# Routing logits without transposes: a fused attention and mixture-of-experts layer on one core

## Chip, core and metric

One core of a Trainium2 chip runs the whole program. The time is device microseconds (us) of that core, as the median of several executions. The kernel keeps five engines busy by hand: TensorE (PE), VectorE (DVE), ScalarE (ACT), GpSimd (POOL), and SyncE (SP), which issues nearly all transfers. They meet only at semaphores.

## Reference

The input is `x` of 4 x 2048 tokens and 256 numbers a token. Everything below starts from the normalised rows.

```python
xn = layernorm(x)
attn = attention over the 16 heads of one token, with biases            # A: per token
h  = rmsnorm(xn, g1);  y = xn + softmax(q k^T) v @ Wo                   # B: causal, 16 heads
t  = rmsnorm(y, g2) = y * r * g2,   r = 1 / sqrt(mean(y*y) + 1e-6)      # C: routing
logits = t @ gate_w;  top_v, top_i = top_k(logits, 2);  gates = softmax(top_v)
moe = sum over the two chosen experts of gate * (silu(t @ w1[e]) @ w2[e])
out = x + attn + y + moe
```

## The kernel before, in words

The program has four stages, one after the other.

- **Projections** (`phase1_project`): 16 chunks of 512 tokens. A chunk is normalised, transposed through PE and projected; one of the products is `heads_ps` (query, key and value columns of part A, 3 x 256 of them, in `head_rows`), which `take_heads` on DVE scales, biases and moves to `heads`. DVE, POOL and ACT make the low parts and statistics beside it.
- **Causal attention** (`phase2_attend`): 16 units of four heads. It leaves the output `o` in memory. The last unit's division by the row sums is left over for the next stage.
- **Routing** (`route`): again 16 chunks, n = 0 to 15, on four token tiles of 128 rows each. For a chunk, PE multiplies `oT` by `wo` (`project`, into `mla_ps`), DVE adds `xn` and has `x2` (the y above), ACT squares it (`squares`), POOL makes `rrms` (the r above, `inverse_rms`), DVE scales to `th` (the t above, `scale_rms`), and ACT copies it (`copy_th`), since each row goes to two experts. Before the change PE also transposes `th` (`transpose_th`), ACT copies the transposed rows (`copy_tT`), and PE multiplies them by `gate_w` (`logits_of`). DVE then picks the two largest logits, PE counts ranks within the experts with triangular and all-ones matrices (`ranks`), DVE turns them to row positions `pos`, and POOL sends the rows to `sorted_rows` with eight indirect transfers a chunk.
- **Experts** (`experts`): 71 tiles of 256 sorted rows, each through two products, added to the output by indirect transfers.

Within routing each engine runs its own list, with work for later chunks placed in it: while chunk n is being ranked, the inputs of chunk n + 2 are made. The lists before are a loop over the first three batches (4 chunks an iteration) and a written-out last batch. The order within a list is that of the code, so a wait holds everything behind it on the same engine. SP's list holds, between the loads and the stores, the last unit's quotients (`scatter_inverse`, `load_raw`, `store_quotient`, with a multiplication of `raw` by `spread` on POOL between them) and the zero rows behind the experts' rows (`blank`).

POOL's part before the loop and in it:

```python
            inverse_rms(0)
            inverse_rms(1)
            wait_apart(pool, last_quotient, RAW_LANDED, apart)
            nc.gpsimd.tensor_tensor(raw[:, :], raw[:, :], spread[:, :], ALU.mult).then_inc(last_quotient, 1)

            def body(b, c, n, ahead):
                if ahead >= 2:
                    inverse_rms(n + 2)
                wait_apart(pool, th_copied, n + 1, apart)
                wait_apart(pool, pos_done, n + 1, apart)
```

## Time and profile before

| | us |
|---|---|
| median of 3 runs | 2802.31 (2799.14 to 2805.09) |
| profiled execution | 2787.22 |
| its span, first to last instruction | 2785.5 |
| PE busy | 2507.4 (90%) |
| DVE busy | 2173.4 (78%) |
| POOL busy | 2140.7 (77%) |
| ACT busy | 1588.1 (57%) |

Stages are read from where their instructions start. Projections run to about 411 and attention from 423.8 to 1963; routing's PE work starts at 1965.7, and the experts' first load is issued at 2217.8. Every share above is a mean over stages with different limits, so the table says nothing on what one stage is worth. That is read from the stage's own rows. In rows, p_ stands in front of tile names, p_small_ps holds the ranks, p_x is x2 in routing, p_g is g2 there, and rows_by_expert is sorted_rows.

### The profile page before, as it was taken

How to read it: one execution, taken by the hardware profiler on the slowest of the kernel's cores; microseconds unless marked ns; L12 is line 12 of the kernel's file. 1: busy time of each engine (PE TensorE's matmuls, PEld its weight loads, DVE VectorE, ACT ScalarE, POOL GpSimd, SP SyncE). 2: the span in 40 equal slices, each digit the busy share in tenths (PEclk: the TensorE clock that was granted, in tenths of full speed). 3: DMA queues.
4: the chain of work that ended last, by engine and by line, in shares of the span. 5: the costliest groups of instructions: out<-in, count | busy, mean ns of one | idle time of the engine just before them, and what ended most of it. 6: DMA issues, size and time to landing. Idle time of an engine off the chain costs nothing. (4 is left out here: it accounts for less than half of the span.)

```text
span 2785.5 us, 57388 instructions
## 1 busy us (share of the span) xinstructions
PE 2507.4 (90%) x21356; PEld 1283.6 (46%) x21356; DVE 2173.4 (78%) x3704; ACT 1588.1 (57%) x2397; POOL 2140.7 (77%) x1245
## 2 busy tenths in 40 slices
PE   7998988999999999999999999999677399999995
PEld 3554443333333333333333333322466288888884
DVE  4557868999899899989999998980266379999980
ACT  2322215677777777777777777778444245555551
POOL 5543338999999999999999999994267556676664
PEclk9999999999999999999999999999777599999997
DMA  5786553223233223322333332211586556565554
GB/s 163 243 252 202 174 174 91 59 73 91 70 86 97 63 81 88 90 73 75 95 69 88 82 91 68 69 38 36 157 280 204 166 118 132 129 133 127 132 118 83
DMA packets 235167, 324.48 MB, mean 116 GB/s; under 512 B 31544, under 2 KB 174744, under 8 KB 234392
## 3 DMA queue, kind: packets, MB, share of 16 engines
q1 hardware_dynamic: 207544, 283.08, 35.6%
q0 software_dynamic: 27360, 37.91, 7.3%
q8 instruction: 163, 2.67, 0.4%
q14 instruction: 100, 0.82, 0.1%
HBM read 238.57 MB, written 145.39 MB: 138 GB/s over the span
## 5 line engine op out<-in xcount | busy, mean ns | idle before, releaser
L1055 DVE TENSOR_REDUCE p_piece_max<-p_ring 128x1 f32<-128x512 f32 (+3 forms) x2160 | 1291.5, 653 | 135.9 <-PE p_ring L164 62.9
L1118 ACT ACTIVATE p_probs<-p_st 128x1024 f32<-128x1024 f32 (+3 forms) x1280 | 1080.7, 897 | 410.7 <-PE p_st L1181 213.9
L1181 PE MATMUL p_st<-unit_q,unit_k 64*128 64x512 bf16 (+3 forms) x3520 | 432.3, 347 | 32.7 <-ACT p_probs L1118 16.8
L1199 PE MATMUL p_pv<-p_probs,unit_vg 128*32 128x512 f32 (+3 forms) x3520 | 410.0, 540 | 0.0
L1869 POOL DMA_INDIRECT out<-p_y,p_rows x142 | 223.0, 1571 | 165.3 <-ACT p_y L1988 100.5
L985 POOL TENSOR_TENSOR p_terms<-p_head_in 128x4096 f32<-128x4096 f32 x38 | 336.1, 8845 | 4.9 <-DMA p_head_in<-head_qkv 4.8
L1012 POOL TENSOR_TENSOR p_terms<-p_head_p,p_head_in 128x4096 f32<-128x4096 f32 x38 | 335.9, 8840 | 0.0
L989 POOL TENSOR_TENSOR p_terms<-p_terms 128x2048 f32<-128x2048 f32 (+2 forms) x114 | 299.6, 2628 | 8.9
L1016 POOL TENSOR_TENSOR p_terms<-p_terms 128x2048 f32<-128x2048 f32 (+2 forms) x114 | 299.5, 2627 | 8.9
L177 PE MATMUL p_ring<-unit_k,unit_q 64*128 64x512 bf16 (+3 forms) x1600 | 271.2, 352 | 32.8 <-DVE p_piece_max L1055 30.3
L2013 PE MATMUL p_hid_ps<-p_rT,p_w 128*128 128x256 f32 x1136 | 259.9, 382 | 3.8 <-DMA p_w<-ffn_w 3.8
L2025 PE MATMUL p_y_ps<-p_w,p_hid 128*128 128x256 f32 x1136 | 257.0, 379 | 0.7 <-ACT p_hid L1976 0.7
L177 PEld LDWEIGHTS p_ring<-unit_k,unit_q 64*128 64x128 bf16 x1600 | 71.3, 93 | 368.4 <-DVE p_piece_max L1055 356.0
L2013 PEld LDWEIGHTS p_hid_ps<-p_rT,p_w 128*128 128x128 f32 x1136 | 217.9, 192 | 34.4 <-issue 4.2
L1181 PEld LDWEIGHTS p_st<-unit_q,unit_k 64*128 64x128 bf16 x3520 | 136.1, 94 | 207.9 <-ACT p_probs L1118 121.2
L2025 PEld LDWEIGHTS p_y_ps<-p_w,p_hid 128*128 128x128 f32 x1136 | 210.4, 190 | 26.6 <-issue 0.9
L1181 PE MATMUL p_st<-p_q,p_k 34*128 34x512 bf16 (+7 forms) x1600 | 194.2, 346 | 8.2 <-ACT p_probs L1118 7.1
L1199 PE MATMUL p_pv<-p_probs,p_vg 128*32 128x512 f32 (+3 forms) x1600 | 186.3, 540 | 0.0
L1856 POOL TENSOR_TENSOR p_pv<-p_pr,p_qkv 128x1024 f32<-128x1024 f32 (+2 forms) x64 | 147.7, 2308 | 30.5 <-ACT p_q_ps L1968 30.5
L1468 POOL DMA_INDIRECT rows_by_expert<-p_th,p_pos x128 | 127.5, 996 | 37.6 <-issue 37.2
L1976 ACT ACTIVATE p_hid<-p_hid_ps 128x512 f32<-128x512 f32 x142 | 84.7, 597 | 114.6 <-PE p_hid_ps L2013 114.3
L177 PE MATMUL p_ring<-p_k,p_q 64*128 64x512 bf16 (+3 forms) x800 | 135.2, 351 | 13.1 <-DVE p_piece_max L1055 11.7
(192 smaller groups left out, 3377.8 us busy)
## 6 DMA issues: line engine op xcount, KB each, us to landing
p_w<-ffn_w SPq DMA_DIRECT2D x142, 512.0 KB
qk_parts<-p_parts SPq DMA_DIRECT2D x64, 384.0 KB, 3.8
head_qkv<-p_heads SPq DMA_DIRECT2D x16, 1536.0 KB, 6.7
p_rows<-rows_by_expert SPq DMA_DIRECT2D x71, 258.0 KB, 3.1
unit_q<-qk_parts SPq DMA_DIRECT2D x132, 128.0 KB, 3.2
unit_k<-qk_parts SPq DMA_DIRECT2D x132, 128.0 KB, 3.7
v_padded<-p_vx SPq DMA_DIRECT2D x16, 1024.0 KB, 8.0
p_head_in<-head_qkv SPq DMA_DIRECT2D x38, 384.0 KB, 3.8
```

The costliest lines, as they stand in the source:

```text
L177: last[half] = nc.tensor.matmul(banks[half][:, k * width:(k + 1) * width], q6[rows, h + k, i * P:(i + 1) * P], k6[rows, h + k, pc * CT:pc ...
L985: step(nc.gpsimd.tensor_tensor(terms[:, :, :, :], head_in[:, slot, 0, :, :].unsqueeze(2).to_broadcast([P, H, H, DH]), head_in[:, slot, 1, ...
L989: step(nc.gpsimd.tensor_tensor(terms[:, :, :, 0:width], terms[:, :, :, 0:width], terms[:, :, :, width:2 * width], ALU.add))
L1012: step(nc.gpsimd.tensor_tensor(terms[:, :, :, :], head_p[:, u, :, :].unsqueeze(2).to_broadcast([P, H, DH, H]), head_in[:, m % 3, 2, :, :]. ...
L1016: step(nc.gpsimd.tensor_tensor(terms[:, :, :, 0:width], terms[:, :, :, 0:width], terms[:, :, :, width:2 * width], ALU.add))
L1055: nc.vector.tensor_reduce(piece_max[:, n % 2, h:h + heads, i, pc], ring_ps[g % RING][:, 0:heads * width].rearrange("p (h k) -> p h k", h=h ...
L1118: nc.scalar.activation(probs[:, 2 * turn_of(s, i) + u, :, 0:width], st_ps[u][:, :, 0:width], ACT.Exp).then_inc(probs_done, 1)
L1181: last = nc.tensor.matmul(st_ps[u][:, half, 0:width], k6[s][rows, PAIR * second + u, kt * P:(kt + 1) * P], q6[s][rows, PAIR * second + u, ...
L1199: last = nc.tensor.matmul(pv_ps[hh * VW:(hh + 1) * VW, skip:CT], vg[s][:, kt, hh * VW:(hh + 1) * VW], probs[:, 2 * turn_of(s, i) + hh % PA ...
L1869: nc.gpsimd.indirect_dma_start(acc, bass.IndirectOffsetOnAxis(rows[:, n % RB, t, D + 1:].bitcast(U32), 0), y[:, n % RB, t, :], None, bound ...
L2013: last = nc.tensor.matmul(hid_ps[i][:, f * ROW_TILE:(f + 1) * ROW_TILE], w1[:, u, k, (2 * i + f) * P:(2 * i + f + 1) * P], rT[:, k, :], st ...
L2025: last = nc.tensor.matmul(y_ps[t][:, 0:D], hid[:, f, t * P:(t + 1) * P], w2[:, n % 2, f, :], start=f == 0, stop=f == FB - 1)
```

## The change

What it does, stage by stage:

1. **Logits as columns.** The logits of a token are `r * (y @ (g2 * gate_w))`, and y is `xn + o @ Wo`. So `xn`'s share comes out of projections, as 8 more columns of `wh` (the rms factor that `take_heads` applies undoes the normalisation of `h`), and POOL copies it to `gate_x`. The other share comes from 8 more columns of `wo`, filled with `gate_o = Wo @ (g2 * gate_w)`, which PE makes at the end of projections. In routing DVE adds the two; the two largest are picked before r is applied, and r multiplies only their difference.
2. **Gone from routing**: the transposes, their copies on ACT, the logit products, the copy of logits out of PSUM, and one of two POOL instructions in `inverse_rms` (the mean and epsilon are now in the scale of the squares and a 257th column of `x2`).
3. **Ranks** are five products of 40 columns in place of 14 of 8.
4. **Lists.** The loop is written out for all 16 chunks. `scale_rms` runs one chunk later, behind `pos` of the chunk before. `inverse_rms(n + 2)` stands behind the transfers of chunk n. `project` is split around `ranks`. The steps of the last unit's quotients stand at chunks 0, 1, 3 and 7 of SP's list (the multiplication at chunk 3 of POOL's), the blank rows at chunks 8 to 14.
5. **Projections** reuse x's buffer for the squares, so a load of x waits for them, and load `g2`, `gate_w` and, at the end, `Wo`.

The core of the diff:

```diff
@@ projections @@
+        gate_o = keep("gate_o", [P, KD, E])
+        gate_x = keep("gate_x", [P, B * NC * TT, E])
-        wh = sb("p1_wh", [P, KD, 3, D])
+        wh = sb("p1_wh", [P, KD, 3 * D + E])
+                sp.dma_start(g2[:, :], w["ffn_g2"].rearrange("(k p) -> p k", p=P)).then_inc(w_loaded, 16)
+            sp.dma_start(wh[:, :, 3 * D:], w["ffn_gate_w"].rearrange("(k p) n -> p k n", p=P)).then_inc(w_loaded, 16)
...
-            wait_apart(sp, xn_done, 1, apart)
+            wait_apart(sp, ss_done, 1, apart)
             load_x(0, 2)
...
                 if not follows:
+                    wait_apart(sp, ss_done, B * NC, apart)
+                    sp.dma_start(x[:, (NC - 1) % 2, 0:KD, :], w["ffn_Wo"].rearrange("(k p) n -> p k n", p=P)).then_inc(wo_loaded, 16)
...
                 lower_parts(n, c % 2, 3)
+                wait_apart(pool, heads_taken, TT * n + TT, apart)
+                nc.gpsimd.tensor_copy(gate_x[:, bass.ds(n * TT, TT), :], heads[:, c % 2, :, 3 * D:]).then_inc(gate_taken, 1)
...
-            dve.wait_ge(w_loaded, 16 * 11)
+            dve.wait_ge(w_loaded, 16 * 13)
             for k in range(KD):
+                last = nc.vector.tensor_scalar(wh[:, k, 3 * D:], wh[:, k, 3 * D:], g2[:, k:k + 1], None, ALU.mult)
...
-                    last = nc.tensor.matmul(heads_ps[:, 2 * D:3 * D], hT[:, s, k, t * P:(t + 1) * P], wh[:, k, 2, :],
+                    last = nc.tensor.matmul(heads_ps[:, 2 * D:3 * D + E], hT[:, s, k, t * P:(t + 1) * P], wh[:, k, 2 * D:],
                                             start=k == 0, stop=k == KD - 1)
@@ routing, all engines @@
-            with eng.Fori(0, B - 1) as b:
+            for b in range(B):
                 for c in range(NC):
-                    body(b, c, NC * b + c, NC)
-            for c in range(NC):
-                body(B - 1, c, NC * (B - 1) + c, NC - 1 - c)
+                    body(b, c, NC * b + c, min(NC, ALL - 1 - NC * b - c))
@@ routing, SyncE @@
-            wait_apart(sp, last_inverse, INVERTED, apart)
-            scatter_inverse(sp, inverse, inverse_of, UNITS - 1, last_inverse)
-            wait_apart(sp, last_inverse, INVERSE_STORED, apart)
-            load_raw(sp, raw, spread, sums_of, inverse_of, UNITS - 1, last_quotient)
-            wait_apart(sp, last_quotient, DIVIDED, apart)
-            store_quotient(sp, o, raw, UNITS - 1, last_quotient)
-            wait_apart(sp, last_quotient, QUOTIENT_STORED, apart)
...
+                quotients_of_last(n)
+                if 8 <= n < 8 + E - 1:
+                    store_blank(n - 8)
@@ routing, GpSimd @@
-                nc.gpsimd.tensor_scalar(rrms[:, :], ss[:, :], 1.0 / D, EPS_RMS, ALU.mult, ALU.add).then_inc(rms_steps, 1)
-                wait_apart(pool, rms_steps, 2 * n + 1, apart)
-                nc.gpsimd.tensor_tensor(rrms[:, :], rrms[:, :], half[:, :], ALU.pow).then_inc(rms_steps, 1)
+                nc.gpsimd.tensor_tensor(rrms[:, c, :], ss[:, :], half[:, :], ALU.pow).then_inc(rms_done, 1)
...
-                if ahead >= 2:
-                    inverse_rms(n + 2)
+                if n == 3:
+                    wait_apart(pool, last_quotient, RAW_LANDED, apart)
+                    nc.gpsimd.tensor_tensor(raw[:, :], raw[:, :], spread[:, :], ALU.mult).then_inc(last_quotient, 1)
                 wait_apart(pool, th_copied, n + 1, apart)
                 wait_apart(pool, pos_done, n + 1, apart)
...
+                if ahead >= 2:
+                    inverse_rms((c + 2) % NC, n + 2)
@@ routing, VectorE @@
-            dve.wait_ge(small_loaded, 32)
+            dve.wait_ge(small_loaded, 16)
...
                     dve.wait_ge(mla_done, 2 * n + i + 1)
+                    nc.vector.tensor_tensor(logits[:, c, 2 * i:2 * i + 2, :], mla_ps[i][:, :, D:D + E],
+                                            gate_x[:, bass.ds(n * TT + 2 * i, 2), :], ALU.add)
...
-                dve.wait_ge(logit_done, n + 1)
-                link(nc.vector.tensor_copy(logits[:, :, :], logit_ps))
+                wait_apart(dve, x2_done, 2 * n + 2, apart)
...
-                nc.vector.tensor_tensor(diff[:, :], top[:, :, 1], top[:, :, 0], ALU.subtract).then_inc(diff_done, 1)
+                link(nc.vector.tensor_tensor(between[:, :], top[:, :, 1], top[:, :, 0], ALU.subtract))
+                nc.vector.tensor_tensor(diff[:, :], between[:, :], rrms[:, c, :], ALU.mult).then_inc(diff_done, 1)
...
+                if ahead >= 1:
+                    scale_rms(*after(b, c + 1), n + 1)
                 if ahead >= 2:
+                    add_attention(*after(b, c + 2), n + 2)
                     add_x(*after(b, c + 2), n + 2)
-                    scale_rms(*after(b, c + 2), n + 2)
@@ routing, TensorE @@
             def body(b, c, n, ahead):
-                logits_of(n)
                 if ahead >= 2:
-                    project(*after(b, c + 2), n + 2)
-                if ahead >= 1:
-                    transpose_th((c + 1) % NC, n + 1)
+                    project(*after(b, c + 2), n + 2, 0)
                 ranks(n)
+                if ahead >= 2:
+                    project(*after(b, c + 2), n + 2, 1)
```

On GpSimd, at the start of routing, these rows stand before; the last three of them are in the loop.

```order
L1446 AFFINE_SELECT p_before<-p_ones 128x128
L1452 TENSOR_SCALAR p_rrms<-p_ss 128x4
L1454 TENSOR_TENSOR p_rrms<-p_rrms,p_minus_half 128x4
L1452 TENSOR_SCALAR p_rrms<-p_ss 128x4
L1454 TENSOR_TENSOR p_rrms<-p_rrms,p_minus_half 128x4
L1459 TENSOR_TENSOR p_raw<-p_raw,p_spread 128x1024
...
L1452 TENSOR_SCALAR p_rrms<-p_ss 128x4
...
L1454 TENSOR_TENSOR p_rrms<-p_rrms,p_minus_half 128x4
...
L1468 DMA rows_by_expert<-p_th,p_pos 69376x258 x8
```

The same place after the change:

```order
L1489 AFFINE_SELECT p_before<-p_ones 128x128
L1495 TENSOR_TENSOR p_rrms<-p_ss,p_minus_half 128x4 x2
L1507 DMA rows_by_expert<-p_th,p_pos 69376x258 x8
L1495 TENSOR_TENSOR p_rrms<-p_ss,p_minus_half 128x4
L1507 DMA rows_by_expert<-p_th,p_pos 69376x258 x8
L1495 TENSOR_TENSOR p_rrms<-p_ss,p_minus_half 128x4
L1507 DMA rows_by_expert<-p_th,p_pos 69376x258 x8
L1495 TENSOR_TENSOR p_rrms<-p_ss,p_minus_half 128x4
L1502 TENSOR_TENSOR p_raw<-p_raw,p_spread 128x1024
L1507 DMA rows_by_expert<-p_th,p_pos 69376x258 x8
```

The quotient's multiplication has moved from ahead of the first eight transfers to behind the third eight, and one instruction stands between two groups of transfers where there were two.

On SyncE, between the loads of the first chunks and the loop, these rows stand before (four pairs of L143 and L144; p_sums and later rows belong to the last unit's quotients):

```order
L132 DMA p_sums<-o_with_sums 32x64 x4
L1374 DMA p_oT_in<-o_heads 128x2x512
L1375 DMA p_x_in<-attn_x 128x4x256
L1370 DMA p_attn<-attn_rows 128x2x256
L136 DMA o_inverse_sums<-p_inverse 128x64
L143 DMA p_raw<-o_with_sums 32x1024
L144 DMA p_spread<-o_inverse_sums 32x1x1024
...
L149 DMA o_heads<-p_raw 128x1024
L1403 DMA out<-p_res 128x4x256
L1409 DMA rows_by_expert<-p_blank 128x2x258 x7
```

The same place after:

```order
L1404 DMA p_oT_in<-o_heads 128x2x512
L1405 DMA p_x_in<-attn_x 128x4x256
L1400 DMA p_attn<-attn_rows 128x2x256
L1425 DMA out<-p_res 128x4x256
L1404 DMA first_oT<-o_heads 128x2x512
L1405 DMA first_x<-attn_x 128x4x256
L1400 DMA p_attn<-attn_rows 128x2x256
L1425 DMA out<-p_res 128x4x256
L136 DMA o_inverse_sums<-p_inverse 128x64
```

The first stores of results and the loads of the fifth chunk (into first_oT and first_x) now come ahead of the quotients' transfers, where they came behind them and behind the seven blank blocks.

## Rows read from the trace of the kernel before

**Rows 1.** Busy time by engine in three stretches: projections, routing, experts.

```profile
core 0: us, PE busy (x) PEld busy (x) DVE busy (x) ACT busy (x) POOL busy (x), PEclk, DMA share, GB/s
30.00:50.00 20.00, 19.75 (x64) 11.06 (x63) 11.70 (x27) 6.77 (x17) 10.29 (x13) 1.00 0.54 172
...
2007.80:2212.00 204.20, 127.55 (x738) 109.19 (x738) 118.85 (x528) 78.44 (x213) 152.76 (x154) 0.71 0.71 221
...
2260.00:2300.00 40.00, 40.00 (x199) 35.24 (x198) 37.51 (x24) 21.17 (x39) 28.25 (x17) 1.00 0.61 147
```

**Rows 2.** Chain that ended last (start, us, what): one expert product.

```profile
2236.38 3.45 PE p_hid_ps L2013 x16
```

**Rows 3.** Timeline of POOL over one routing chunk (start, us, instruction, [idle before]).

```profile
2106.54 1.26 POOL L1468 DMA_INDIRECT rows_by_expert<-p_th,p_pos  x1 [0.20 <-issue]
...
2116.73 1.07 POOL L1452 TENSOR_SCALAR p_rrms<-p_ss 128x4 f32<-128x4 f32 x1
2117.98 1.04 POOL L1454 TENSOR_TENSOR p_rrms<-p_rrms,p_minus_half 128x4 f32<-128x4 f32 x1 [0.18 <-POOL p_rrms L1452]
2119.22 1.26 POOL L1468 DMA_INDIRECT rows_by_expert<-p_th,p_pos  x1 [0.20 <-issue]
```

**Rows 4.** Two routing lines of POOL: duration ns min/median/max, first and last start.

```profile
L1468 POOL DMA_INDIRECT rows_by_expert<-p_th,p_pos x128: 956/961/1274, 2007.8 to 2211.0; - x128
...
L1452 POOL TENSOR_SCALAR p_rrms<-p_ss x16: 191/800/1125, 1982.0 to 2179.4; 128x4 f32<-128x4 f32 x16
```

**Rows 5.** Timeline at the start of routing.

```profile
1970.04 1.10 SPq L1382 DMA_DIRECT2D p_g<-ffn_g  x1
...
1978.09 0.69 DVE L1488 TENSOR_TENSOR first_x<-first_x,p_attn 128x512 f32<-128x512 f32 x1 [10.61 <-DMA p_gate_w<-ffn_gate_w]
...
1980.13 6.67 PE L1671 MATMUL p_mla_ps<-wo,p_oT_in 128*128 128x256 f32 x16 [9.07 <-DVE p_x L1493]
...
2003.80 2.34 POOL L1459 TENSOR_TENSOR p_raw<-p_raw,p_spread 128x1024 f32<-128x1024 f32 x1 [12.29 <-DMA p_spread<-o_inverse_sums]
...
2007.82 1.27 POOL L1468 DMA_INDIRECT rows_by_expert<-p_th,p_pos  x1 [0.21 <-issue]
```

**Rows 6.** Transfers issued from 1960 to 1990: KB, us to landing.

```profile
p_g<-ffn_g SPq DMA_DIRECT2D x1, 128.0 KB, 5.0
```

**Rows 7.** DVE's waits from 2045 to 2195: us in total, times, longest.

```profile
DVE p_th L1501 <- POOL p_rrms L1454: 14.6, 11, 1.4
```

**Rows 8.** Timeline of DVE over one routing chunk.

```profile
2045.07 0.18 DVE L1532 COPY p_logits<-p_logit_ps 128x32 f32<-128x32 f32 x1
...
2047.48 0.19 DVE L1545 TENSOR_TENSOR p_either<-p_chosen 128x32 bf16<-128x32 f32 x1
...
2049.28 0.69 DVE L1488 TENSOR_TENSOR p_x_in<-p_x_in,p_attn 128x512 f32<-128x512 f32 x1 [1.60 <-ACT p_xn L1615]
...
2051.08 0.16 DVE L1551 TENSOR_SCALAR p_denom<-p_ediff 128x4 f32<-128x4 f32 x1
...
2053.50 1.23 DVE L1512 TENSOR_TENSOR p_res<-p_x_in,p_x 128x1024 f32<-128x1024 f32 x1
...
2056.03 1.67 DVE L1501 SCALAR_TENSOR_TENSOR p_th<-p_x,p_rrms,p_g 128x256 f32<-128x256 f32 x4 [1.31 <-POOL p_rrms L1454]
```

**Rows 9.** Timeline at the end of routing.

```profile
2195.95 9.58 SPq L1426 DMA_DIRECT2D rows_by_expert<-p_blank  x8
...
2211.03 0.96 POOL L1468 DMA_INDIRECT rows_by_expert<-p_th,p_pos  x1 [0.30 <-issue]
2217.83 0.40 SPq L1831 DMA_DIRECT2D p_rows<-rows_by_expert  x1
```

**Rows 10.** The value-column product's line, and timeline at both ends of projections.

```profile
L687 PEld LDWEIGHTS p_heads_ps<-p_wh,p_hT x256: 190/190/190, 27.4 to 409.6; 128*128 128x128 f32 x128
...
13.79 0.43 DVE L535 TENSOR_SCALAR p_wh<-p_wh 128x512 f32<-128x512 f32 x1 [3.67 <-DMA p_rest<-attn_bv]
...
18.07 1.09 PE L641 MATMUL p_t<-ident,p_h 128*128 128x128 f32 x4 [18.07 <-DVE p_h L491]
...
423.86 1.04 PE L1181 MATMUL p_st<-unit_q,unit_k 64*128 64x512 bf16 x4 [12.80 <-SPq L933]
```

More of the change, by code:

```diff
@@ L211, in phase1_project @@
         SHARED["chunks"] = (x_v, w)
+        gate_o = keep("gate_o", [P, KD, E])
+        gate_x = keep("gate_x", [P, B * NC * TT, E])
+        SHARED["routing"] = (gate_o, gate_x)
         row_stats = SHARED["row_stats"] = keep("row_stats", [P, 2, B * NC * TT])
@@ L583, in _ @@
             chunks(dve, body)
+            dve.wait_ge(part2_done, 4 * B * NC)
+            dve.wait_ge(gate_steps, 2)
+            nc.vector.tensor_copy(rest[:, 0, :], t_ps[:, :]).then_inc(gate_steps, 1)
+            dve.wait_ge(gate_steps, 4)
+            nc.vector.tensor_copy(gate_o[:, :, :], cv_ps[:, 0:KD * E].rearrange("p (k e) -> p k e", e=E)).then_inc(gate_steps, 1)
         @block.scalar
@@ L591, in squares @@
                 for t in range(TT):
[L592 removed]
+                    last = nc.scalar.activation(x[:, s, t, :], xn[:, s, t, :], ACT.Square, accum_out=ss[:, t:t + 1])
                 last.then_inc(ss_done, 1)
@@ L732, in _ @@
             chunks(pe, body)
+            pe.wait_ge(maxima_steps, 4)
+            pe.wait_ge(wo_loaded, 16)
+            for j in range(KD):
+                for i in range(KD):
+                    last = nc.tensor.transpose(t_ps[:, j * D + i * P:j * D + (i + 1) * P], x[:, (NC - 1) % 2, i, j * P:(j + 1) * P],
+                                               ident[:, :])
+            last.then_inc(gate_steps, 1)
+            pe.wait_ge(gate_steps, 3)
+            pe.wait_ge(vx_done, 2 * B * NC)
+            for i in range(KD):
+                for j in range(KD):
+                    last = nc.tensor.matmul(cv_ps[:, i * E:(i + 1) * E], rest[:, 0, j * D + i * P:j * D + (i + 1) * P], wh[:, j, 3 * D:],
+                                            start=j == 0, stop=j == KD - 1)
+            last.then_inc(gate_steps, 1)
 def phase2_attend(nc, apart, qk_heads, v_units, o, head_qkv, attn_rows, first_units):
@@ L1245, in route @@
     row_stats = SHARED["row_stats"]
-    ident = SHARED["consts"][0]
+    gate_o, gate_x = SHARED["routing"]
     attn_rows = SHARED["attn_rows"]
@@ L1288, in route @@
         chosen = sb("p3_chosen", [P, TT, 2, E])
-        either = sb("p3_either", [P, TT, E], BF16)
+        either = sb("p3_either", [P, 2 * TT + 1, E], BF16)
+        between = sb("p3_between", [P, TT])
         diff = sb("p3_diff", [P, TT])
@@ L1620, in squares @@
             def squares(n):
[L1622 removed]
+                act.wait_ge(rms_done, n)
                 act.wait_ge(x2_done, 2 * n + 2)
                 for t in range(TT):
[L1625 removed]
+                    last = nc.scalar.activation(sq[:, t, :], x2[:, t, :], ACT.Square, scale=D ** -0.5, accum_out=ss[:, t:t + 1])
                 last.then_inc(ss_done, 1)
[L1628 to L1633 removed]
             def copy_th(b, c, n):
```

187 lines of the change are left out of this document (85 added, 102 removed).

## The prediction

> **What bounds the kernel now.** I read the busy time of stretches first [rows 1]. The reader is to see three stages with different limits. In projections PE is busy 19.75 of 20 us, in the experts 40 of 40. In routing no engine is: PE 127.6 of 204.2 us, DVE 118.9, POOL 152.8, and the clock that TensorE is granted is 0.71. Then I read the chain of what ended last. From the experts' start it is PE product after PE product, 3.45 us for 16 records [rows 2], with no wait on routing's data. So the experts take what they take from their first load, and a microsecond by which routing ends earlier is a microsecond off the total.
>
> What paces routing shows in POOL's timeline [rows 3]. Transfers of one chunk start at 2106.54 and those of the next at 2119.22: 12.68 us. Eight transfers fill 10.19 of it (2106.54 to 2116.73). An indirect transfer is busy 0.96 us [rows 4] and the next starts 0.30 after its end, so POOL's "idle" of that kind is part of the price. The rest is the two instructions of `inverse_rms` and 0.20. POOL has no other gap, so it bounds the stage although it counts as 75% busy. DVE waits for it: 1.31 us ahead of `th` in the chunk shown [rows 8], 14.6 us in 11 chunks [rows 7].
>
> The last view is the start [rows 5]. The first transfer goes out at 2007.82. Its inputs were ready before that; POOL stood 12.29 us waiting for `p_spread`, multiplied for 2.34, and only then came to the chunk. And DVE's first addition, at 1978.09, waited for the small `gate_w` load, not for the projections.
>
> **The change part by part, routing.**
>
> *Start.* `gate_w` is no longer waited for; `g2` was issued at 1970.04 and takes 5.0 to land [rows 5, 6], so DVE starts at 1975.1. From the addition of attention to the end of x2 it needs 1.8 (2049.28 to 2051.08 [rows 8]), and two new additions of [128, 2, 8] logits about 0.25 each, by the small rows of that chunk: 1977.4. PE's second projection has been waiting for this and takes 6.67 us [rows 5], 6.9 with 264 columns for 256: 1984.3. The copy of `gate_o`, for which PE's first projection now waits, is DVE's first instruction and hidden, since the first projection has until 1976. The last half of x2 takes 0.9 more, the result's addition 1.2: 1986.4. From the first logit instruction to `either` it was 2.6 (2045.07 to 2047.67); the copy goes (0.33) and a chained subtraction and a first wait come (0.33 and 0.15): 2.8 to 2.95. From `denom` to `pos` 2.4 (2051.08 to 2053.50), which covers PE's ranks. So `pos` stands at 1991.7 and the first transfer at 1991.9, 15.9 earlier. `th` of chunk 0 is ready long before.
>
> *Pace.* One POOL instruction and the wait behind it go: 2116.73 to 2117.98, 1.25 us. The chunk becomes 11.4. Fourteen chunks have one, so 17.8 in all (14 x 1.27 with the rounding of both periods).
>
> *Moved multiplication.* It now costs POOL 2.4 us ahead of the transfers of chunk 3, near 2026. Its data is issued at SP's chunk 1, near 1996, and took some 8 us from there before, so no wait is added. SP stands at its chunk 3 until the multiplication is over, near 2028; behind it wait the store of result 5 and loads for chunk 8, needed two chunks later or more.
>
> *Stalls at the start.* Fourteen periods of 12.68 and two of 10.15 from 2007.82 end at 2205.6, yet the last transfer ends at 2211.99 [rows 9]. The 6.4 missing were lost in the first chunks, where SP sent the blocked results' stores and seven blank blocks in one burst. With these spread I count them as gone.
>
> Sum for the stage: 1991.9 + 14 x 11.4 + 2.4 + 2 x 10.15 = 2174.2, against 2211.99: 37.8 us earlier.
>
> *Does another engine take over?* DVE's period before, 2045.07 to 2057.62, held waits of 1.60 and 1.31 [rows 8]; 9.65 is work. Added: two logit additions 0.5, the chained step, less the copy, 0.15 to 0.3. That gives 10.4 of 11.4. The 1.60 wait was for ACT's `xn`, asked for late in the new list. PE has 6.9 of projection even at 1.2 GHz (its lower level, which the end of routing shows), and about 0.5 of ranks. ACT loses 1.1 of copies. None reaches 11.4. In the loop POOL's power, `th`, x2, squares, next power, DVE and ACT need about 7 us of the 11.4; from the power to `pos` of the same chunk about 10.8, which is the tightest.
>
> *End.* SP's eight tail stores took 9.58 us from 2195.95 and were over long before POOL [rows 9]. Now they start about 8 us after the transfers of chunk 14 begin and end near 18, while POOL ends at 20.3. They stay covered by 2 us; the 5.8 us from POOL's end to the first expert load stay.
>
> **Projections.** Here the change costs. Two more small transfers stand ahead of the weights on which DVE waits until 13.79, in a queue that is full, and PE's first work at 18.07 hangs directly on it [rows 10]: 2 issues of 0.5 and a little transfer time, between 0.5 and 3, taken 1.3. The value columns grow from 256 to 264. A record of 256 columns takes 3.45 / 16 = 0.216 us [rows 2], there are 256 of them [rows 10], so 8/256 of 55 us is 1.7; PE is the bound in half of the stage, taken 1.4. DVE's `take_heads` grows by 1%, 0.3. At the end one more issue, 0.5, stands ahead of SP's last stores, for which PE waits 12.80 us [rows 10]. The new transposes and products of `Wo` fall into that wait (about 4 us of work after a load of about 6); without that cover they would cost 4. The later load of x (now behind the squares) has a chunk of slack. The new copy to `gate_x` on POOL waits for the fourth `take_heads`, behind which nothing is ready earlier, as DVE makes the next moments after it. Sum 3.5, between 1 and 8.
>
> **Total.** The profiled execution of 2787.2 would become 2787.2 - 37.8 + 3.5 = 2752.9, 34.3 less. It lies 15 under the median of the runs, and the same difference taken from the median gives 2802.3 - 34.3 = 2768.0.
>
> **Two neighbours on one port.** POOL's small instruction took 0.19 at best and 1.12 at worst [rows 4]; the long ones run beside DVE's 1.23 us addition of two tiles and end with it (2053.50 to 2054.73 in rows 8). The Trainium skill, "GPSIMD Engine Reference", section Key points, says that POOL shares its SBUF interfaces with VectorE and contends with DVE instructions of two SBUF inputs. The trace agrees. By that rule the sum depends on where the remaining power lands, which is the first rival.
>
> **Rivals.**
>
> 1. *The power is delayed instead.* If it meets DVE's two-input instructions each time, it pays what its predecessor paid, 0.93, and the pace is 12.3. Gain 34.3 - 13 = 21, time 2781. Against it: DVE should stand waiting for the power, as `scale_rms` now comes directly behind it. For it: DVE has only 1 us to spare, and if it lags it is in the addition. 12%.
> 2. *The pace stays.* A loop of DVE, PE and ACT, or transfers. The transfer engines are 0.71 busy over the stage [rows 1], so 0.79 at the new pace, and loads and stores may land late; or written-out lists cost in fetching code. The early start is kept: 34.3 - 17.8 = 16.5, time 2786. 10%.
> 3. *Slower.* POOL's wait for `heads_taken` in projections holds its low parts, DVE waits for these, and PE for DVE. It would have to cost 2.4 us in each of 16 chunks (37.8/16) to cancel the gain; at 3.5 us a chunk the kernel takes 56 - 37.8 more, 2821. Against it: PE is busy 19.75 of 20, POOL only 10.3 [rows 1], and the order of DVE's list. 5%.
> 4. *No change.* The experts' end is not moved by their start, or some other end of routing holds them: 2802. Against it: the chain. 3%.
>
> **How the numbers follow.** My forecast has 70%, with a range of its own from 2757 (projections at 1, start 5 us better, pace 11.2) to 2776 (projections at 8, stalls half kept). Rivals 1 and 2 lie at 2781 and 2786. The range 2757 to 2786 leaves out the slower and unchanged cases, 8%, and the outer tails of the others, about 12%. A measurement of this kernel tells 0.2% (5.6 us) from no change: faster 92%, same 3%, slower 5%.
>
> **What would show it.** POOL's first routing transfer 15.9 us earlier relative to the end of attention; starts of neighbouring chunks' first transfers 11.4 apart with a power of 1.04; DVE waiting for it about 1 us in each chunk; projections longer by 3 or 4 us, PE's first work by 1.3. Wrong it would be if powers take 2 us, if DVE never waits for POOL, if PE starts attention over 8 us late, or if the tail stores end after POOL.

## The result, and the profile after

The changed kernel takes 2762.55 us (2758.78 to 2763.58, 4 runs); beside it the kernel before took 2803.7 (2799.14 to 2808.98, 4 runs). The ratio is 0.985 [0.983, 0.987], 41 us less. The forecast was 2768.0 in a range of 2757 to 2786. The two profiled executions tell another size: spans of 2785.5 and 2761.8 us, 23.7 apart. The first question is where 23.7 come from, the second where the other 17 are.

Stretches of the changed kernel, as [rows 1] has them of before:

```profile
core 0: us, PE busy (x) PEld busy (x) DVE busy (x) ACT busy (x) POOL busy (x), PEclk, DMA share, GB/s
30.00:50.00 20.00, 19.74 (x64) 10.93 (x63) 11.75 (x26) 6.76 (x17) 10.72 (x14) 1.00 0.54 177
1995.20:2187.30 192.10, 81.00 (x283) 56.53 (x283) 124.18 (x562) 68.33 (x194) 151.77 (x143) 0.72 0.74 229
2240.00:2280.00 40.00, 40.00 (x197) 35.24 (x196) 37.55 (x21) 21.74 (x42) 27.14 (x16) 1.00 0.61 143
```

PE lost 47 us of busy time in routing and 455 records, and the stage from the first transfer to the last lost 12. What sets the pace is POOL's timeline, one chunk of it with DVE beside it:

```profile
2069.49 1.04 POOL L1495 TENSOR_TENSOR p_rrms<-p_ss,p_minus_half 128x4 f32<-128x4 f32 x1
2070.57 1.67 DVE L1545 SCALAR_TENSOR_TENSOR p_th<-p_x,p_rrms,p_g 128x256 f32<-128x256 f32 x4 [2.33 <-POOL p_rrms L1495]
2070.74 1.23 POOL L1507 DMA_INDIRECT rows_by_expert<-p_th,p_pos  x1 [0.20 <-issue]
2072.16 0.68 DVE L1530 TENSOR_TENSOR first_x<-first_x,p_attn 128x512 f32<-128x512 f32 x1
2072.27 1.41 POOL L1507 DMA_INDIRECT rows_by_expert<-p_th,p_pos  x1 [0.30 <-issue]
2073.99 0.96 POOL L1507 DMA_INDIRECT rows_by_expert<-p_th,p_pos  x1 [0.30 <-issue]
2074.30 1.22 DVE L1556 TENSOR_TENSOR p_res<-first_x,p_x 128x1024 f32<-128x1024 f32 x1
2075.25 1.10 POOL L1507 DMA_INDIRECT rows_by_expert<-p_th,p_pos  x1 [0.30 <-issue]
...
2081.45 1.04 POOL L1495 TENSOR_TENSOR p_rrms<-p_ss,p_minus_half 128x4 f32<-128x4 f32 x1
2082.53 0.88 DVE L1545 SCALAR_TENSOR_TENSOR p_th<-p_x,p_rrms,p_g 128x256 f32<-128x256 f32 x2 [2.31 <-POOL p_rrms L1495]
2082.69 1.23 POOL L1507 DMA_INDIRECT rows_by_expert<-p_th,p_pos  x1 [0.20 <-issue]
```

The reader is to see three things against [rows 3]. The chunk lasts 11.96 us (2069.49 to 2081.45), no longer 12.68. The power stands clean at 1.04. And the eight transfers fill 10.71 us (2070.74 to 2081.45), where they filled 10.19: the first, second and fourth took 1.23, 1.41 and 1.10. DVE waits 2.33 us for the power, against 1.31 [rows 8]; in eleven chunks it is this row, the successor of [rows 7]:

```profile
DVE p_th L1545 <- POOL p_rrms L1495: 25.1, 11, 2.3
```

The start, for [rows 5]:

```profile
1972.10 0.48 SPq L1412 DMA_DIRECT2D p_g<-ffn_g  x1
...
1979.44 0.69 DVE L1530 TENSOR_TENSOR first_x<-first_x,p_attn 128x512 f32<-128x512 f32 x1 [9.39 <-DMA p_g<-ffn_g]
...
1995.25 1.27 POOL L1507 DMA_INDIRECT rows_by_expert<-p_th,p_pos  x1 [4.07 <-issue]
```

and the end, for [rows 9]:

```profile
2173.82 9.64 SPq L1467 DMA_DIRECT2D rows_by_expert<-p_blank  x8
...
2186.29 0.96 POOL L1507 DMA_INDIRECT rows_by_expert<-p_th,p_pos  x1 [0.30 <-issue]
2194.64 0.41 SPq L1844 DMA_DIRECT2D p_rows<-rows_by_expert  x1
```

Projections, for the timelines in [rows 10]:

```profile
17.80 1.08 PE L664 MATMUL p_t<-ident,p_h 128*128 128x128 f32 x4 [17.80 <-DVE p_h L505]
...
425.95 1.04 PE L1219 MATMUL p_st<-unit_q,unit_k 64*128 64x512 bf16 x4 [5.09 <-SPq L971]
```

From one trace to the other, stage by stage: attention starts 2.1 us later (423.86 to 425.95), and it ends 0.3 later on top (POOL's first routing instruction stands at 1965.49 before and 1967.86 now). From there to the first transfer it was 42.3 us and is 27.4 (-14.9). The transfers from first to last start took 203.2 and take 191.0 (-12.2). From the last transfer's end to the experts' first load it was 5.84 and is 7.39 (+1.55). The sum is -23.2 of the 23.7.

The 12.2 us of the transfers are not spread evenly. Counted between the first transfers of neighbouring chunks, the first three periods took 48.4 us and take 39.8 (-8.6), the next ten took 125.2 and take 119.4 (-5.9, which is 12.52 and 11.94 a chunk), and the last two took 20.8 and take 23.0 (+2.2).

### The profile page after: what moved, and what is told of

The parts are those of the page before. It is cut to its first block and busy times, and to the rows that moved or that the text cites. A ratio compares the mean times of both kernels' runs of the same rounds, so it can differ in the third digit from the quotient of the medians.

```text
span 2761.8 us, 55901 instructions
## 1 busy us (share of the span) xinstructions
PE 2451.8 (89%) x20840; PEld 1221.1 (44%) x20840; DVE 2178.1 (79%) x3741; ACT 1573.7 (57%) x2365; POOL 2139.1 (77%) x1248
## 5 line engine op out<-in xcount | busy, mean ns | idle before, releaser
L1507 POOL DMA_INDIRECT rows_by_expert<-p_th,p_pos x128 | 134.8, 1053 | 44.0 <-issue 40.2
L622 ACT CAST p_parts<-p_qk 128x512 bf16<-128x512 f32 x64 | 37.5, 586 | 192.9 <-PE p_qk L693 97.7
```

## The experiments

They ran on three chips, four kernels each, always with the kernel before beside them. The kernel before took 2809.8 us on the first, 2808.3 on the second and 2784.8 on the third. That is itself a finding, to which the section below returns.

### Repeat the kernel before, and take the change apart (first chip)

`e1_before_again` is the kernel before, unaltered.

> The kernel before, unchanged, with a trace of its own from the chip on which the next three run. It is here because the two traces differ by 23.7 us of span, while the medians differ by 41. Theory 'burst': the profiled execution of before was a lucky one, and the 15 us to its median lie in the first chunks of routing, where SP sends seven blank blocks at once; then a trace near the median shows the stretch from 2007 to 2045 longer and all else as it was. Theory 'elsewhere': the 15 us are spread over attention or the experts, or belong to another chip; then routing takes 204 us again and the ratio to the median is nothing that the change did there. Ratio to before 1.000 by both.

Measured: 2808.58 us, ratio 1.0001 [0.9992, 1.0010]; its trace has a span of 2807.9 us, 22.4 more than the first trace of the same program. Attention starts 1.6 later and lasts 3.3 longer; the transfers of routing take 218.5 us for 203.2, and the way from the last one to the experts 10.5 for 5.8. The 15 in the transfers are no burst at the start. They lie in chunks of 13.5 to 14.0 us between others of 12.4 to 13.1 over the whole stage (13.33 in the mean of the ten where the first trace has 12.52) and in a last one of 14.9, with a wait that the first trace has nowhere. DVE's waits from 1990 to 2230, in which "remote" means that the wait was ended by a semaphore's update with no record of an instruction that fits it:

```profile
DVE p_place L1561 <- remote: 25.7, 9, 4.9
...
DVE p_logits L1532 <- remote: 5.6, 1, 5.6
```

One of these waits in the timeline:

```profile
2053.37 0.24 PE L1704 MATMUL p_small_ps<-p_either,p_ones 128*128 128x8 bf16 x4
...
2060.46 0.19 DVE L1561 TENSOR_TENSOR p_place<-p_small_ps,p_base 128x32 f32<-128x32 f32 x1 [2.82 <-remote]
```

PE's last record of the ranks is over at 2053.61, and `p_place`, which beside them needs only what its own engine has made, starts 6.85 us later. DVE is free for it from 2057.64, so 2.82 us are lost. Nor is it the ranks alone: from 2054.63 to 2060.42 this trace has no record of an update of a semaphore by any engine, although 16 instructions that make one started in that time.

`e2_projections_alone` has the new projections (the 8 columns of the gate, g2, `gate_x`, `gate_o`) and the old `route`, which ignores what they made.

```diff
-        wh = sb("p1_wh", [P, KD, 3, D])
+        wh = sb("p1_wh", [P, KD, 3 * D + E])
...
+        gate_o = keep("gate_o", [P, KD, E])
+        gate_x = keep("gate_x", [P, B * NC * TT, E])
```

> Projections as after the change (8 more columns, gate_x, gate_o, the loads), routing as before: its results gate_x and gate_o are made and not used. Theory of the prediction: this part costs 3.5 us (1 to 8). The trace of after has 2.1 us more up to the start of attention, so I now expect +2 to +3 us. Rival: the part costs nothing or gains, because loads of x now come later and DVE and ACT meet less; then the time is that of before within 1 us. A cost above 6 us would mean that the waiting copy on POOL hurts.

Measured: 2811.12 us, ratio 1.0000 [0.9989, 1.0011]. In the traces attention starts at 426.10, 0.6 after `e1`, and PE's first work is at 17.95, 0.35 earlier. The projections' part costs less than can be measured: the interval reaches 3 us to either side of nothing.

`e3_lists_alone` is the kernel before with the loop written out and the last unit's quotients, POOL's long multiplication and the blank rows at their new places.

```diff
-            with eng.Fori(0, B - 1) as b:
+            for b in range(B):
...
-            for i in range(E - 1):
+            def store_blank(i):
...
+                quotients_of_last(n)
+                if 8 <= n < 8 + E - 1:
+                    store_blank(n - 8)
```

> The kernel before with only the lists changed: routing's loop written out, the last unit's quotients at chunks 0, 1, 3 and 7, the multiplication at chunk 3 on POOL, blank rows at chunks 8 to 14. Logits still go through transposes. By the sum over the traces: first transfer 5.6 us earlier (pos of chunk 0 was ready at 2002.0 and the transfer went at 2007.8), 6.4 us of stalls gone, 2.4 paid at chunk 3: 9 to 10 us faster than the profiled before, and if theory 'burst' holds, up to 25 us faster than the median of before. Rival: the lists bring nothing alone, since POOL's pace of 12.7 stays and the burst was harmless: within 3 us of before.

Measured: 2795.77 us, ratio 0.9950 [0.9937, 0.9964], 14 less. The late ranks are still there (22.9 us in 7 waits). What went is in this row of the first trace of the kernel before, DVE's waits from 1990 to 2230:

```profile
DVE p_res L1512 <- DMA out<-p_res: 16.9, 2, 10.3
```

DVE could not write the third and fourth residual (waits of 10.31 and 6.57 us), since the first one's store stood in SP's list behind the quotients, issued at 2009.23, and the second one's behind the blank rows, at 2020.19, from where it took until 2029.91 to land. `e3` and the changed kernel have no such row.

`e4_lists_undone` is the changed kernel with those lists put back as they were; only the loop stays written out.

> The kernel after with the quotient steps, their multiplication and the seven blank blocks back at the start of routing, all else changed. The reciprocal of the sums goes back ahead of DVE's loop too. By the traces: the first transfer waits for the multiplication again, some 7 us later than after, 2.4 us are saved at chunk 3, and the burst's stalls of 3 to 6 come back: 8 to 11 us slower than after, so about 30 us faster than the median of before. If theory 'burst' holds in full, it is 20 us or more slower than after. Rival (spreading is worth nothing): within 2 us of after.

Measured: 2778.16 us, ratio 0.9885 [0.9869, 0.9900], 31.6 less than before. Its steady chunks come 11.95 us apart as in the changed kernel, DVE again waits for the stores of the residual (22.3 us, 2), and early in the stage two powers stand 22.6 us apart.

### What a transfer waits for, and what is late (second chip)

`f1_after_again` is the changed kernel, unaltered.

> The changed kernel unaltered, as the base for the runs beside it. Theory: 0.985 of the kernel before, some 2763 to 2770 us, with chunks of routing 11.96 us apart. Rival: the difference of the first two traces (2785.5 to 2761.8 us of span) is the real one, then 0.991 of the kernel before.

Measured: 2763.39 us, ratio 0.9843 [0.9831, 0.9856]: 45 us less than before on this chip, at nearly the time that it had in the first comparison. Its span is 2759.6 us, and no wait of DVE in routing is ended by "remote".

`f2_ranks_alone` is the kernel before with the new form of the ranks.

```diff
-                for t in range(TT):
-                    nc.tensor.matmul(rank_ps[:, t, :], before[:, :], either[:, t, :], start=True, stop=t == 0)
...
+                nc.tensor.matmul(rank_ps, before[:, :], either[:, TT:, :], start=True, stop=False)
+                for t in range(1, TT + 1):
+                    last = nc.tensor.matmul(rank_ps, ones[:, :], either[:, TT - t:2 * TT + 1 - t, :], start=False, stop=t == TT)
```

> The kernel before with only the ranks of the changed kernel: 5 products over padded columns where there are 14. In the repeated runs of the kernel before, VectorE gets the ranks 1 to 7 us after TensorE's last record of them, and every second chunk or so lasts 14 instead of 12.6 us; in the first trace of it and in the changed kernel this does not occur in the steady chunks. Theory A (the 14 small products are what is late): the waits of p_place vanish and the time falls by about 15 us, to 0.9947 of before. Theory B (what stands before the ranks in TensorE's order is late, the transposes, the logits): the waits stay, and the time falls by no more than 3 us, 0.999 to 1.000.

Measured: 2802.11 us, ratio 0.9980 [0.9970, 0.9990], 6 less, with single runs from 2797 to 2810. The waits of `p_place` fell from 25.7 us in 9 to 15.2 in 6. But the profiled execution was the slowest of the twelve, 7.5 us above their median, on another chip than `e1`, and has other waits of the kind (4.5 us for `p_count_i`, 4.4 for `p_logits`). So the count of waits shows little. Neither theory holds: the new form of the ranks is worth some 6 us and does not make the late semaphores go.

`f3_one_input` is the changed kernel with one addition altered; the attention's share is missing from its output.

```diff
-                nc.vector.tensor_tensor(x[c][:, 0:2, :], x[c][:, 0:2, :], attn[:, c, :, :], ALU.add).then_inc(attn_added, 1)
+                nc.vector.tensor_scalar(x[c][:, 0:2, :], x[c][:, 0:2, :], 1.0, None, ALU.add).then_inc(attn_added, 1)
```

> The changed kernel with VectorE's addition of the attention rows (two inputs in SBUF, 0.68 us) replaced by an addition of a constant to the same tile; the attention's share is left out of the output. Theory (a transfer is slowed while VectorE runs an operation with two SBUF inputs): the second transfer of a chunk falls from 1.41 towards 0.96 us, the first (beside scale_rms, 1.23) and the fourth (beside the residual's addition, 1.10) stay, the pace falls from 11.96 to about 11.5 and the time by 5 to 7 us against the changed kernel on this chip. Rival (the copies on ScalarE or the loads by DMA slow the transfers): 1.41 us stays and the time changes by less than 2 us.

Measured: the pace is 11.67 us and the second transfer 1.14, from 1.41. The operation itself fell from 0.68 to 0.42:

```profile
2073.80 0.42 DVE L1530 TENSOR_SCALAR first_x<-first_x 128x512 f32<-128x512 f32 x1
2073.92 1.14 POOL L1507 DMA_INDIRECT rows_by_expert<-p_th,p_pos  x1 [0.30 <-issue]
```

The time, 2764.13 us, is that of `f1` within its uncertainty (ratio 0.9841): in its trace the transfers take 186.1 us for 188.6, but attention starts 2.5 later and the experts last 2.4 longer; whether the edit has to do with either is not shown. The theory as written is half wrong, and the 5 to 7 us that it promised did not come. It is not the two inputs that stretch the transfer; an operation with one stretches it as well, by less as it is over sooner.

`f4_power_on_act` makes the power on ACT.

```diff
-                nc.gpsimd.tensor_tensor(rrms[:, c, :], ss[:, :], half[:, :], ALU.pow).then_inc(rms_done, 1)
+                nc.scalar.activation(lnss[:, :], ss[:, :], ACT.Ln).then_inc(ss_done, 1)
+                nc.scalar.activation(rrms[:, c, :], lnss[:, :], ACT.Exp, scale=-0.5).then_inc(rms_done, 1)
```

> The changed kernel with the power taken from GpSimd and made by ScalarE as exp(-ln(mean square) / 2), right behind the squares. Theory (POOL's queue of eight transfers and the power is the bound, the power is on it with 1.04 us and its handing over with 0.20): the pace falls from 11.96 to 10.7 us, and the time by 15 to 18 us against the changed kernel on this chip, about 2748. Rival 1 (VectorE's chain is next, with 9.63 us of work and its waits): pace 11.3, time 8 us less. Rival 2 (ScalarE loads its tables for ln and exp by turns, twice or more in a chunk, and the ratio's exp comes late): pace 12 or more, time the same or longer.

Measured: 2777.42 us, ratio 0.9893 [0.9878, 0.9907], 14 slower than `f1`. Rival 2 holds in its first half:

```profile
2071.03 0.96 POOL L1502 DMA_INDIRECT rows_by_expert<-p_th,p_pos  x1 [0.30 <-issue]
2071.08 1.23 DVE L1549 TENSOR_TENSOR p_res<-p_x_in,p_x 128x1024 f32<-128x1024 f32 x1
...
2072.84 1.28 ACT L1664 ACT_TABLE_LOAD   x1
2074.13 0.20 ACT L1664 ACTIVATE p_lnss<-p_ss 128x4 f32<-128x4 f32 x1
2074.44 1.28 ACT L1666 ACT_TABLE_LOAD   x1
```

Two table loads of 1.28 us a chunk stand ahead of the exponential that `p_denom` needs. But they do not make every chunk longer. By PE's ranks, chunks of 9.5 to 10.7 us alternate with chunks of 14 to 17, and in the long ones waits of DVE are ended by "remote" here too (8.0 us in 3 for `p_between`). So the late semaphores are not a matter of the old chunk alone.

The first two rows serve another question: a transfer that started 0.05 us *before* the residual's addition took its 0.96, though the addition ran beside it all the way, and the addition its 1.23.

### Use it, and the rest of the list (third chip)

`g1_rows_first` moves one operation in DVE's list. `add_rows` is the addition of the attention rows, taken out of `add_attention`.

```diff
+                if ahead >= 2:
+                    add_rows(*after(b, c + 2), n + 2)
                 if ahead >= 1:
                     scale_rms(*after(b, c + 1), n + 1)
```

> The changed kernel with one operation moved in VectorE's order: the addition of the attention rows of chunk n + 2 stands ahead of scale_rms of chunk n + 1, in the 2.3 us in which VectorE waits for the power, and no longer behind it. Theory (a transfer that GpSimd starts while VectorE is inside an operation with two inputs in SBUF waits for the end of that operation, and is not slowed once begun): the second transfer of a chunk falls from 1.41 to 0.96 us, the fourth from 1.10 to 0.96, the first (beside scale_rms) stays at 1.23; the pace falls from 11.96 to 11.4 us and the time by 6 to 8 us against the changed kernel, a ratio of about 0.9818 to before where the changed kernel had 0.9843. Rival 1 (the traces' 1.41 us has another cause, the loads or ScalarE's copy beside it): 1.41 stays, and the ratio. Rival 2 (other transfers then meet the residual's addition): the sum of the eight stays at 10.7 us.

Measured: 2758.79 us, ratio 0.9907 [0.9892, 0.9922] to a kernel before of 2784.8. A chunk, with DVE's operations beside it:

```profile
2070.95 1.67 DVE L1547 SCALAR_TENSOR_TENSOR p_th<-p_x,p_rrms,p_g 128x256 f32<-128x256 f32 x4 [1.93 <-POOL p_rrms L1495]
2071.12 1.23 POOL L1507 DMA_INDIRECT rows_by_expert<-p_th,p_pos  x1 [0.20 <-issue]
2072.66 0.96 POOL L1507 DMA_INDIRECT rows_by_expert<-p_th,p_pos  x1 [0.30 <-issue]
...
2074.26 1.23 DVE L1558 TENSOR_TENSOR p_res<-first_x,p_x 128x1024 f32<-128x1024 f32 x1
...
2075.18 1.13 POOL L1507 DMA_INDIRECT rows_by_expert<-p_th,p_pos  x1 [0.30 <-issue]
...
2080.14 0.69 DVE L1530 TENSOR_TENSOR p_x_in<-p_x_in,p_attn 128x512 f32<-128x512 f32 x1
2080.42 1.25 POOL L1507 DMA_INDIRECT rows_by_expert<-p_th,p_pos  x1 [0.30 <-DVE p_pos L1611]
```

The second transfer is at 0.96, as the theory said, and rival 2 took most of it back: the addition now stands where the eighth starts, 1.25. The pace is 11.80 for 11.96, 2 us in 13 chunks where 6 to 8 were expected.

`g2_rows_first_and_late_g2` adds the later wait for g2.

```diff
-            dve.wait_ge(small_loaded, 16)
             LINKS = 10
...
             add_x(0, 0, 0)
+            dve.wait_ge(small_loaded, 16)
             scale_rms(0, 0, 0)
```

> As the run before, and VectorE's wait for the gains g2 moved from the front of its first chunk to the first scale_rms, which is what reads them. In the changed kernel VectorE's first addition waited 9.3 us for that load, until 7.3 us after its issue. Theory: VectorE starts at the landing of the first attention rows, about 4 us earlier, and the first transfer comes 3 to 4.4 us earlier; 3 to 4 us less than the run before. Rival: the attention rows or ScalarE's second normalization (which waits 8.2 us for the second chunk's rows) land as late as g2, and it is worth less than 1 us.

Measured: 2757.28 us, ratio 0.9903 [0.9888, 0.9919], 1.5 less than `g1`, which is inside the uncertainty. In the traces DVE starts 7.9 us into the stage, where it was 11.5 in `f1`, but the first transfer comes at 26.5 for 28.2. ACT's second normalization waits for the second chunk's rows, 8.7 us, and what depends on it is the path from there. The rival is nearly right: 1.7 of 4 are left.

`g3_unrolled_alone` is the kernel before with its loop written out and nothing else.

> The kernel before with its loop over the chunks written out and nothing else changed: the quotients and the blank rows stay where they were. The lists and the written-out loop together gave 14 us. Theory (the gain came from the steps moved out of SyncE's and GpSimd's start): within 3 us of before. Rival (the loop's own branches and registers cost it): 5 to 14 us less than before.

Measured: 2781.72 us, ratio 0.9994 [0.9985, 1.0003]. So, as far as a run on another chip can tell, it was the moved steps that gave `e3` its 14 us. DVE waits for the residual's stores as before (15.7 us, 2).

`g4_few_stores` is the kernel before, storing 16 of 128 partitions of each residual; seven eighths of that part of the output are missing.

```diff
-                sp.dma_start(out_v[b, c], res[:, c % 2, :, :]).then_inc(res_stored[c % 2], 16)
+                sp.dma_start(out_v[b, c][0:16], res[0:16, c % 2, :, :]).then_inc(res_stored[c % 2], 16)
```

> The kernel before, with only 16 of 128 partitions of each residual chunk stored, so that most of the residual is left out of the output. It tests the late arrivals of TensorE's ranks on VectorE in the repeated traces of the kernel before (0.6 to 7 us behind TensorE's record of them). Theory A (they are late because the DMA engines are full: 448 of some 2,800 KB a chunk go): the waits of p_place for something that the profile does not tell vanish, chunks come 12.6 us apart and the time falls by 12 us or more. Theory B (they have to do with the old chunk's work on the engines): the waits stay, and the time falls by less than 5 us.

Measured: 2784.16 us, ratio 0.9997 [0.9988, 1.0006]. The experiment says nothing on its question, because there was nothing to remove: neither this trace nor that of `g3`, both with the old chunk on this chip, has one wait of DVE ended by "remote" in routing. What it does say is that the 448 KB a chunk that it leaves out cost nothing where nothing is late.

## Why the prediction was right, and where its steps were not

**The mechanism was right.** Routing's start and POOL's pace held the experts, and a microsecond there was one off the total. The start came out within 1 us of its term; the pace gave less than half of its own. Put together on the trace's own scale, the forecast was 10.7 us too good (2752.9 for a profiled 2763.58). On the scale of the medians it was 5.5 too bad. The forecast lies in its range because of two errors of opposite sign, and that is luck.

**Start.** Forecast 15.9 earlier, measured 14.9. The load of g2 landed 7.3 us after its issue, not 5.0 [rows 6], and so DVE began 11.6 us into the stage for a forecast of 9.6; the rest of the chain was 1.0 shorter than worked out. The step took it that a landing time of the kernel before would hold. Why the load takes longer now was not tried; in `e3`, with the new lists and the old loads, it landed after 5.0.

**Pace.** Forecast 11.4, measured 11.96; over 14 chunks 7.8 us of the shortfall. The step that failed is the one that kept the eight transfers at 10.19 us. I had seen in [rows 4] and [rows 8] that POOL's small instruction ran long beside DVE's addition, and asked only what the *power* would meet. That was rival 1, and its place was wrong: the power met nothing (1.04), the transfers did. What they pay follows a rule. An instruction of POOL that starts inside one of DVE's two long additions in SBUF (of the attention rows, and of the residual) ends later by what was left of the addition, less 0.12 to 0.15 us. If it has started before the addition, or in its first few hundredths of a us, it pays nothing. In the traces of the changed kernel this covers all 25 such starts of the first and all 26 of `f1`. Beside the four short operations of `scale_rms`, and where they follow the addition at once, it is not so exact: the first transfer of a chunk pays 0.27 there (1.23 for 0.96).

| run | POOL starts | DVE's operation ends | left | longer by |
|---|---|---|---|---|
| changed, 2nd transfer | 2072.27 | 2072.84 | 0.57 | 0.45 |
| changed, 4th | 2075.25 | 2075.52 | 0.27 | 0.14 |
| `f3`, 2nd | 2073.92 | 2074.22 | 0.30 | 0.18 |
| `g1`, 4th | 2075.18 | 2075.49 | 0.31 | 0.17 |
| `g1`, 8th | 2080.42 | 2080.83 | 0.41 | 0.29 |
| `e1`, power | 2073.51 | 2074.41 | 0.90 | 0.76 |
| `f4`, transfer | 2071.03 | (addition starts 2071.08) | - | 0 |

The case of `e1`, from its timeline (the rows of `f4` stand with its run):

```profile
2073.18 1.23 DVE L1512 TENSOR_TENSOR p_res<-p_x_in,p_x 128x1024 f32<-128x1024 f32 x1
2073.51 1.80 POOL L1454 TENSOR_TENSOR p_rrms<-p_rrms,p_minus_half 128x4 f32<-128x4 f32 x1 [0.18 <-issue]
```

The Trainium skill says in "SBUF — State Buffer", section "SBUF: two separate sides", that the pair of ports which VectorE and GpSimd share is a lock: of a GpSimd operation and a VectorE operation with two SBUF inputs or in a two-port mode, whichever starts first holds it for the whole instruction. The table agrees for POOL. The other half is seen here too, but only beside POOL's long multiplication, at its new place:

```profile
2032.56 2.33 POOL L1502 TENSOR_TENSOR p_raw<-p_raw,p_spread 128x1024 f32<-128x1024 f32 x1
2032.61 3.76 DVE L1545 SCALAR_TENSOR_TENSOR p_th<-p_x,p_rrms,p_g 128x256 f32<-128x256 f32 x4 [2.40 <-POOL p_rrms L1495]
```

`scale_rms` started 0.05 us after the multiplication and took 3.76 us for its usual 1.67; `f1`, `f3`, `g1` and `g2` show the same 3.76. So the moved multiplication holds DVE for 2.1 us as well, which I had not counted. POOL was busy with it for the same time, and the period is longer by 2.3 us in all (`f1`). Beside a transfer DVE is not held: the addition of `f4` that started inside one was not longer, and neither was any of some 800 other additions and operations of `scale_rms` that did so in all the traces. Nor were the seven additions that started inside a power.

The first transfer's 1.23 was there before (1.26 in [rows 3]), so 0.45 and 0.14 are new, and 0.52 of them shows in the period (10.71 for 10.19). With the rule they could have been counted from [rows 8] and the new order of DVE's list before the run.

A second error is in what the term was taken from. The chunk of [rows 3] is one of the longest; ten chunks of the kernel before are 12.52 us apart in the mean, not 12.68. And the old list puts `inverse_rms` between 13 pairs of chunks, not 14, while the new one does so between 14, which is one reason why the last two periods became longer. So the steady chunks gained 0.58 us each for a forecast of 1.27. DVE was no bound, as forecast: 9.6 us of work in 11.96 (2.33 of waiting), where I had 10.4 in 11.4.

**Stalls.** I took 6.4 us as lost to a burst and gone with the new lists. The cause named was roughly right, the size not: `e3`, `g3` and the wait of `p_res` for its stores put the moved steps at 14 us with the old chunk, and `e4` against `f1` at 15 with the new one, on different chips. The 14 or 15 include the multiplication at the start (first transfer 33.7 us into the stage in `e4`, 28.0 in `f1`), which I had booked under "start". The 6.4 itself was too small, because it is what the overrated pace left over: the first two periods before (16.90 and 18.79) lie 10.6 us above two of 12.52. In the traces most of the transfers' gain is here and not in the pace: 8.6 of 12.2 us came from the first three periods, although they now hold the moved multiplication (2.3 us by `f1`, where that period is 14.21 for 11.94) and, in this trace, one late semaphore (2.1 us).

**End and projections.** I expected 5.8 us from POOL's end to the first load to stay; it is 7.4, and 6.9 to 7.9 in `f1`, `g1` and `g2`. Why was not tried. Projections were forecast at +3.5: the traces show +2.1, and `e2` no measurable cost. The time of PE's first work, which I thought 1.3 later, varies from 16.6 to 18.4 us between all the traces, with and without the change, so that term was below what a pair of traces can show.

**The step from the trace to the median.** This is the error worth most, 17 us. I added the same difference to the median, as though the 15 us between profiled execution and median were a constant of the measurement. They are a behaviour: on two chips the kernel before has late ranks and chunks of 14 us, and takes 2808 to 2810; on the third it has none and takes 2785, as in the first trace, 2787.2. The changed kernel had 2762.6 and 2763.4 on chips where the kernel before had 2803.7 and 2808.3. The changed kernel loses little by the late semaphores (2.1 us in one wait in its first trace, none in `f1`), and so gains 41 to 45 us there. On a chip like the third the two spans suggest some 24; the changed kernel itself was not run there, `g1` was, with 26.

The traces themselves fall into two kinds, by how many of the updates that the engines' instructions make are on record. From 2040 to 2170 it is nearly all of them in the first trace of the kernel before (502 of 504) and in the four of the third chip (485 of 487 in `g1`). In the first trace of the changed kernel it is 296 of 472, in `e1` 280 of 476, and 51 to 65% in all eight of the first two chips, with stretches of up to 7.8 us that have none. Every late semaphore is in a trace of this second kind. So the two traces compared at the top were not taken under the same conditions. The record does not say on which chips, but the trace of before is of the kind in which that kernel takes 2785. This fits the 17 us between the two measures of the gain; no run shows it directly.

**What stays open.** Why updates of semaphores come late on two of three chips, and why the old chunk loses so much by it. Each chip was used in one sitting, so chip and time of day are not told apart. It is not a matter of one engine: in `f4` an update of DVE and one of PE are on record at 2024.32 and 2024.34, 4.1 and 3.9 us behind their instructions. Whether the missing records and the late updates have one cause is not shown. The ranks' form is worth little (`f2`), the written-out loop and the lists none that shows (`e3` has the waits), and `f4` shows it in a chunk without transposes. Whether traffic of the DMA engines does it could not be answered where `g4` ran.

**The best version** is `g2`, 2757.28 us. It beats the kernel before by 1.0% on the chip where that is at its fastest. Against the changed kernel the gain is argued from traces (11.81 for 11.96 us a chunk, first transfer 0.9 to 1.5 us earlier), not measured on one chip.

## What to carry to other kernels

When a neighbour's long operation stretches an instruction, ask what will stand at that moment after the change, for every instruction of the engine and not only for the one that was stretched; moving the operation may only move the collision. Take a pace from the mean of many chunks and count the periods in the code; what is misread there turns up as a loss somewhere else. A difference between one trace and the median is a finding to be explained before a forecast carries it over: look for rows that some executions of the same program have and others lack. And a store that waits in a list behind an unrelated job shows up far away, as another engine's wait for its own buffer.

## What the hardware showed that I had not expected

- The same program took 2785 us on one chip and 2808 to 2810 on two others, with ranges of 9 to 10 us each; that of the third chip does not touch the others. The changed kernel took 2762.6 and 2763.4 where that program took 2803.7 and 2808.3, and its variant `g1` 2758.8 on the third.
- On the slower two, results of PE reached DVE up to some 7 us after PE's record of them (6.85 in the timeline of `e1`), and in `f4` single steps between DVE's own instructions waited 1 to 4 us.
- GpSimd waits for the end of VectorE's addition only when it *starts* inside it; a transfer under way is not slowed by one that starts later, nor does it slow that one. GpSimd's multiplication of 128x1024 does: `scale_rms`, started 0.05 us behind it, took 3.76 us for 1.67.
- An operation of DVE on one input in SBUF (0.42 us for 128x512) holds POOL up like one with two (0.68 us).
- Alternating ln and exp on ScalarE costs a table load of 1.28 us each way, for two operations of 0.20 us.
